# One attention and expert layer on one core: stages reordered row by row, pads zeroed up front, gate sums spread by transposes

## The chip, the cores and the metric

The kernel runs on one core of a Trainium2 chip. The core has TensorE (PE, with its weight loads PEld), VectorE (DVE), ScalarE (ACT), GpSimd (POOL) and SyncE (SP). Each of them works through a queue of its own in order, and they wait for each other on semaphores. The metric is the device time in microseconds, lower is better.

## The reference

All data is float32. `x` is 8 rows (b) of 512 tokens (t) of 128 features. Shift, scale and gain of both halves come from `silu(c) @ wmod`, and the two gains are held away from zero.

```
h   = layernorm(x) * (1 + ca) + sa                     # per row b
n   = h * rsqrt(mean(h*h) + 1e-6) * norm_w
q, k, v, o = n@Wq.T/8, n@Wk.T/8, n@Wv.T, sigmoid(n@Wo.T + bo)   # 64 wide
zi, zf = n@wi + bi, n@wf + bf                          # one number per token
scan over t:  m' = max(zf + m, zi)
              C  = exp(zf + m - m') C + exp(zi - m') v k^T ; n likewise
              out_t = o * (C q) / max(|n.q|, 1)
x   = x + ga * (h + out @ Wout.T)
h   = layernorm(x) * (1 + cb) + sb
logits = h @ Wr + br ; the two best of 8 experts, softmax of the two
x   = x + gb * sum_e gate_e * (relu(h@W1[e] + b1[e]) @ W2[e] + b2[e])
```

## The kernel before

**The attention half, row by row.** A row is 4 tiles of 128 tokens. For each row PE transposes the normalized tokens (stage `xT`, line 1213), ACT makes `hT` and its squares `sq`, PE projects (`qk` 1219, `V` 1229, `V3` 1233, the mean square `ms` 1223), DVE copies `kT` (923), POOL takes the root (`rms` 633), DVE makes `vz` (936). The scan over tokens is turned into a 512 x 512 weight matrix: PE sums the forget gates (`F` 1243, 1245), DVE forms `a_col` (943), PE spreads that column over all partitions (`abc` 1254), DVE scans for the running maximum `m_bc` (948) and adds the causal mask (`m_far` 951), ACT exponentiates (`E`), DVE multiplies with the scores (`Pw`, line 906), and PE applies the weights (`pv` 1264). Then `hh`, `hhT`, `proj` (1288), the second norm (`x1`, `ag1`, `rs1`, `xn1`), `x2T` (1294) and the router (`lg` 1301).

**The expert half, two ways.** Rows 0, 6 and 7 are dense: all 8 experts over the whole row (`du` line 1183, `dh` 697, `dd` 1192, `da` 1039; 24 pairs of a row and an expert). Rows 1 to 3 (group 0) and 4, 5 (group 1) are routed. `rank` and `pick` number the tokens of each expert, POOL scatters each token tile twice into `h_slots` in DRAM (`scat`, line 643, 8 per row), and `block_list` on DVE turns the counts into a list of 31 (23) blocks of 128 slots with one expert each. SP loads them four at a time, 14 quads in all: 4 value loads (553), 4 token blocks `xl` (555), 4 weight blocks `wl` (557). PE works through them (`T` 1146, `up` 1157, `dn` 1168), SP stores the results (563), POOL gathers them back (`gat`, line 657), DVE combines (`comb`).

**Zeros.** The last block of each expert is only partly filled. Before, `pads(g)` on SP waits for the counts, then reads 8 addresses with value loads and writes 8 zero blocks of 64 KB behind the filled slots (lines 537 to 540), twice in the program. Only the spare region behind the last expert is zeroed early (line 533).

**What sets the order.** A table `TICK` gives each step of each stage a number; each engine runs a loop over the numbers, issues what is due, and takes stages with the same number in the order of its code. The numbers set an order and nothing else. Which steps can pass each other is limited by the semaphores, and by one PSUM bank being shared by several stages (`bE` by the router, the ranks, the counts and the second norm; `bD` by `abc`, the scores, `pv` and `hhT`).

**The start.** `norm0(n)` is the first norm. It is called three times, for row 0, rows 1 to 3 and rows 4 to 7, each as one run of DVE instructions (`n0s`), followed by a power on POOL (`n0p`) and by activations on ACT for the same rows (`n0a`, line 710). `gain_diag`, `gain_rows` (PE, line 1115), `gain_out` and `gain_sum` spread the gains over partitions.

Of the kernel before, what the change touches and what calls it, by code (L numbers as in the profile page):

```python
# [5 lines left out]
def adaln_mlstm_moe_kernel(  # L6
# [67 lines left out]
    NORM0 = ((0, 1), (1, 4), (4, B))  # L74
    CAP = [len(r) * T + P for r in GROUPS]
# [10 lines left out]
    for g in range(NG):  # L86
        for p in range(0, NB[g], 2):
# [9 lines left out]
    TICK = dict(  # L97
        fill=(),
        gain_p=(47, 82),
        T=(611, 664, 703, 728, 755, 781, 831, 861, 885, 929, 978, 1012, 1038, 1071),  # L100
        up=(632, 635, 682, 685, 710, 714, 737, 740, 763, 766, 806, 820, 837, 841, 869, 873, 912, 915, 938, 941, 990, 994,
            1020, 1024, 1050, 1054, 1080, 1083),
        dn=(646, 677, 700, 705, 723, 730, 749, 757, 797, 800, 823, 833, 857, 866, 882, 889, 961, 964, 974, 987, 1005, 1008,
            1034, 1040, 1076, 1085, 1095, 1099),
        du=(267, 281, 302, 316, 328, 404, 428, 483, 875, 901, 931, 954, 967, 1013, 1027, 1057, 1088, 1113, 1127, 1141, 1155,
            1168, 1182, 1196),
        dd=(292, 309, 345, 365, 393, 416, 455, 494, 891, 922, 945, 980, 997, 1043, 1064, 1103, 1120, 1134, 1148, 1162, 1175,
            1189, 1203, 1216),
# [8 lines left out]
        F=(121, 198, 280, 402, 505, 609, 708, 809),
        S0=(138, 212, 340, 425, 526, 623, 744, 827),
        abc=(125, 202, 323, 411, 514, 613, 717, 814),
        S2=(132, 205, 338, 414, 517, 617, 721, 818),  # L120
        pv=(155, 233, 356, 444, 567, 653, 783, 848),
        hgaT=(164, 288, 372, 462, 576, 676, 791, 908),
        hhT=(175, 290, 374, 464, 587, 689, 804, 910),
        proj=(184, 299, 386, 471, 595, 696, 811, 919),
        x2T=(219, 326, 423, 503, 627, 726, 844, 952),
        lg=(241, 335, 435, 510, 639, 733, 862, 1072),
        h2=(343, 442, 519, 644, 747),
        rank=(354, 452, 533, 662, 760),
        cnt=(543, 773),
        gain_d=(42, 71, 99, 108),  # L130
        hb=(615, 668, 707, 731, 758, 801, 834, 864, 888, 933, 984, 1015, 1041, 1076),
        n0s=(53, 78),
        n0m=(52, 77, 104),
        k=(105, 176, 255, 380, 470, 588, 677, 774),
        mse=(107, 185, 263, 386, 483, 596, 680, 794),
        vz=(113, 192, 269, 393, 493, 602, 689, 803),
        a=(124, 201, 282, 406, 512, 612, 712, 812),
        scan=(133, 207, 328, 419, 521, 618, 723, 822),
# [60 lines left out]
    with ctx:  # L199
# [308 lines left out]
        def _(sp):  # L508
# [849 lines left out]
```

## Time and profile before

| what | before |
|---|---|
| time, median of 3 (lowest to highest) | 337.53 us (334.25 to 339.64) |
| profiled execution: time, span | 336.14 us, 334.3 us |
| PE busy, share of the span | 290.4 us, 87% |
| DVE, ACT, POOL busy | 193.1, 136.7, 107.9 us |
| mean granted TensorE clock | 0.904 |
| DMA traffic | 39.84 MB |

The span is the profiled execution from its first to its last instruction. Busy time of PE contains the slower stretches: a matmul at half the granted clock counts with twice its time. The row "PEclk" of the page shows that clock over 40 slices of the span, in tenths of full speed.

### The profile page before, as it was taken

The page shows a single profiled execution, that of the slowest core. Times are in us where ns is not written, and L with a number is a line of the kernel's source. Part 1 is how long each engine was busy: PE and PEld are TensorE (multiplying, and loading weights), DVE is VectorE, ACT ScalarE, POOL GpSimd, SP SyncE. Part 2 cuts the span into 40 slices and gives each one's busy share as a digit, 9 for nine tenths or more (in the row PEclk, how much of TensorE's full clock was granted, in tenths as well). Part 3 has the DMA queues.
Part 4 walks back from the last instruction along what each step waited for, and adds up shares of the span by engine and source line. Part 5 has one row for each costly group of instructions (what it writes and reads, how often), then busy time and mean ns, then how long its engine had stood idle before and what let it go on. Part 6 is the DMA issues. An engine that isn't in the chain of part 4 may idle for free.

```text
span 334.3 us, 5728 instructions
## 1 busy us (share of the span) xinstructions
PE 290.4 (87%) x1793; PEld 232.7 (70%) x1793; DVE 193.1 (58%) x769; ACT 136.7 (41%) x321; POOL 107.9 (32%) x167
## 2 busy tenths in 40 slices
PE   2662889899999999875989999999799999999992
PEld 2341568486779778645778897978688788886772
DVE  3576325542476776674576676777315565845664
ACT  1147804305462452430262675063451525443430
POOL 8024001101104704717211821730005777007730
PEclk9996557559999999965899999999999999999998
DMA  4893000000000100113246666764666487821312
GB/s 103 252 280 116 0 2 1 0 1 0 2 0 26 40 2 24 41 31 111 86 172 237 219 232 216 258 220 171 202 227 212 149 291 250 269 73 39 85 45 83
DMA packets 43315, 39.84 MB, mean 119 GB/s; under 512 B 4819, under 2 KB 34934, under 8 KB 43286
## 3 DMA queue, kind: packets, MB, share of 16 engines
q1 hardware_dynamic: 40498, 34.11, 31.2%
q0 software_dynamic: 2624, 5.31, 5.8%
q8 instruction: 14, 0.23, 0.3%
q14 instruction: 15, 0.12, 0.1%
q10 hardware_dynamic: 164, 0.07, 0.1%
HBM read 11.50 MB, written 10.22 MB: 65 GB/s over the span
## 4 chain that ended last, share of the span: by engine, by line
PE 53%; SPq 19%; DVE 11%; issue 6%; POOL 4%; DMA 4%; ACT 2%; DVEq 0%; POOLq 0%
PE bank L1192 11%; PE bank L1183 10%; PE bank L1264 6%; SPq L553 5%; SPq L557 4%; SPq L555 4%; PE bank L1123 3%; PE bank L1168 2%; PE bank L1219 2%; PE bank L1157 2%; PE bank L1254 2%; POOL yg L657 2%; SPq L522 2%; PE bank L1288 2%; POOL rstd L626 2%
## 5 line engine op out<-in xcount | busy, mean ns | idle before, releaser
L643 POOL DMA_INDIRECT h_slots<-h2k,slot x40 | 39.3, 983 | 71.7 <-DVE slot L1062 61.5
L657 POOL DMA_INDIRECT yg<-y_slots,y_slot x40 | 39.0, 975 | 57.4 <-DMA y_slots<-yb 46.0
L1192 PEld LDWEIGHTS bank<-w_all,hid_d 128*128 128x128 f32 x384 | 45.4, 192 | 8.0 <-issue 5.6
L1192 PE MATMUL bank<-w_all,hid_d 128*128 128x128 f32 x384 | 47.4, 276 | 2.1 <-DVE acc L1039 1.3
L697 ACT ACTIVATE hid_d<-bank,w_all 128x512 f32<-128x512 f32 x48 | 32.3, 691 | 33.4 <-PE bank L1183 30.5
L1183 PE MATMUL bank<-h2d,w_all 128*128 128x512 f32 x96 | 45.8, 600 | 0.0
L1039 DVE SCALAR_TENSOR_TENSOR acc<-bank,gates,acc 128x128 f32<-128x128 f32 x96 | 27.0, 344 | 26.3 <-PE bank L1192 23.3
L686 ACT ACTIVATE hid<-bank,wl 128x128 f32<-128x128 f32 x108 | 29.9, 378 | 24.4 <-PE bank L1157 23.9
L1123 PE MATMUL bank<-qT,kT 64*128 64x384 f32 (+3 forms) x64 | 28.2, 549 | 7.9 <-DVE kT L923 6.7
L1264 PE MATMUL bank<-vz,ew 128*128 128x65 f32 x160 | 25.6, 330 | 9.2 <-DVE ew L906 9.2
L1264 PEld LDWEIGHTS bank<-vz,ew 128*128 128x128 f32 x160 | 24.6, 244 | 11.7 <-DVE ew L906 11.7
L1157 PE MATMUL bank<-hb,wl 128*128 128x128 f32 x216 | 27.2, 278 | 2.2 <-issue 1.4
L1168 PE MATMUL bank<-wl,hid 128*128 128x128 f32 x216 | 28.6, 277 | 0.0
L1168 PEld LDWEIGHTS bank<-wl,hid 128*128 128x128 f32 x216 | 26.3, 192 | 3.2 <-issue 1.9
L1157 PEld LDWEIGHTS bank<-hb,wl 128*128 128x128 f32 x216 | 25.4, 192 | 4.1 <-issue 2.9
L1183 PEld LDWEIGHTS bank<-h2d,w_all 128*128 128x128 f32 x96 | 16.4, 190 | 12.7 <-issue 12.2
L1123 PEld LDWEIGHTS bank<-qT,kT 64*128 64x128 f32 x64 | 11.7, 214 | 15.2 <-issue 8.5
L633 POOL TENSOR_TENSOR rms<-ms_eps,minus_half 128x4 f32<-128x4 f32 x8 | 8.3, 1034 | 43.3 <-DVE ms_eps L928 43.2
L906 DVE SCALAR_TENSOR_TENSOR ew<-bank,rms,ew 128x512 f32<-128x512 f32 (+3 forms) x32 | 16.2, 545 | 7.4 <-PE bank L1123 3.8
L710 ACT ACTIVATE xn<-x_all,nmr,rstd 128x128 f32<-128x128 f32 x32 | 12.6, 480 | 14.9 <-DVE nmr L920 14.9
L672 ACT ACTIVATE ew<-m_far,a_col 128x128 f32<-128x128 f32 x32 | 12.5, 391 | 10.2 <-DVE m_far L951 10.2
L636 POOL TENSOR_TENSOR rstd<-ve,minus_half 128x4 f32<-128x4 f32 x8 | 8.6, 1071 | 24.0 <-DVE ve L978 23.9
(196 smaller groups left out, 454.6 us busy)
## 6 DMA issues: line engine op xcount, KB each, us to landing
wl<-w_all SPq DMA_DIRECT2D x54, 321.0 KB, 2.8
xl<-h_slots SPq DMA_DIRECT2D x54, 64.0 KB, 1.9
y_slots<-yb SPq DMA_DIRECT2D x12, 256.0 KB, 4.3
x_all<-in_L_attn_x_dram SPq DMA_DIRECT2D x8, 256.0 KB, 5.6
out_dram<-x_all SPq DMA_DIRECT2D x8, 256.0 KB, 2.6
w_all<-in_L_ffn_W_dram SPq DMA_DIRECT2D x1, 1024.0 KB, 7.5
w_all<-in_L_ffn_W_dram SPq DMA_DIRECT2D x2, 512.0 KB, 8.8
h_slots<-zeros SPq DMA_DIRECT2D x16, 64.0 KB, 1.5
```

Source lines behind the costliest of these rows:

```text
L553: words = [sp.value_load(list_w[0:1, q0 + i:q0 + i + 1]) for i in range(n)]
L643: g_.indirect_dma_start(out=h_slots[GROUP_OF[b]], out_offset=bass.IndirectOffsetOnAxis(slot[:, b, i, j:j + 1], 0), in_=h2k[m % 2][:, j, :] ...
L657: g_.indirect_dma_start(out=yg[m % 2][:, j, i, :], out_offset=None, in_=y_slots[GROUP_OF[b]], in_offset=bass.IndirectOffsetOnAxis(y_slot[: ...
L686: last = a.activation(hid[r % 2][:, m, u, :], up_at(r)[:, (m * NU + u) * P:(m * NU + u + 1) * P], ACT.Relu, bias=wl[c % RL][:, i + m, O_B1 ...
L697: a.activation(hid_d[n % 2][:, u, :], dense_banks(b)[u][:, :], ACT.Relu, bias=w_all[:, e, O_B1 + u:O_B1 + u + 1]).then_inc(s_dh, 1)
L1039: last = v.scalar_tensor_tensor(acc[:, j, :], dense_banks(b)[2][:, j * D:(j + 1) * D], gates[n // E % 2][:, j, e:e + 1], acc[:, j, :], ALU ...
L1123: t_.matmul(scores_at(j), kT[:, j * P:(j + 1) * P], qT[:, j * P:T], start=True, stop=True).then_inc(s_S, 1)
L1157: last = t_.matmul(up_at(r)[:, (m * NU + u) * P:(m * NU + u + 1) * P], wl[c % RL][:, i + m, u * P:(u + 1) * P], hb[c % 2][:, i + m, :], st ...
L1168: last = t_.matmul(y_bank[:, (i + m) * D:(i + m + 1) * D], hid[r % 2][:, m, u, :], wl[c % RL][:, i + m, at:at + D], start=u == 0, stop=u = ...
L1183: t_.matmul(dense_banks(b)[u][:, :], w_all[:, e, u * P:(u + 1) * P], h2d[:, :], start=True, stop=True).then_inc(s_du, 1)
L1192: last = t_.matmul(dense_banks(b)[2][:, j * D:(j + 1) * D], hid_d[n % 2][:, u, j * P:(j + 1) * P], w_all[:, e, at:at + D], start=u == 0, s ...
L1264: last = t_.matmul(pv_at(n), ew[:, o:o + P], vz[:, j, 0:NS], start=j == 0, stop=j == n)
```

## The change

All numbers in `TICK` are new, for every stage and engine. `norm0` and `n0a` now work one row at a time, with four semaphores for the loads of x (row 0; row 1; rows 2 and 3; rows 4 to 7) in place of three; the power on POOL stays in three groups. `pads` is gone: SP writes zeros into every slot of both groups early, 18 DMAs behind the weight loads, and the first scatter of each group waits for that group's nine. `block_list` loses the copy of the pad addresses, and its last five instructions become a stage of its own, `places`. `abc` uses transposes in place of matmuls. The rest are waits that the new order needs, and two fill stages that stay empty.

```diff
     TICK = dict(
-        gain_p=(47, 82),
-        list=(547, 777),
-        pads=(548, 798),
+        gain_p=(110, 172),
+        list=(456, 680),
+        places=(486, 952),
...
-            sp.wait_ge(s_w, 16 * (2 + NU))
-            sp.wait_ge(s_lists0, 1)
             sp.wait_ge(s_zero, 1)
             for g in range(NG):
-                sp.dma_start(h_slots[g][E * CAP[g]:SLOTS[g], :].rearrange("(n p) d -> p n d", p=P), zeros[:, :, :].to_broadcast([P, E - 1, D])).then_inc(s_spare, 16)
-
-            def pads(g):
-
-                sp.wait_ge(s_list_p, g + 1)
+
                 for e in range(E):
-                    at = sp.value_load(list_p[0:1, g, e:e + 1])
-                    sp.dma_start(h_slots[g][bass.ds(at, P), :], zeros[:, 0, :]).then_inc(s_pad, 16)
+                    sp.dma_start(h_slots[g][e * CAP[g]:(e + 1) * CAP[g], :].rearrange("(p n) d -> p n d", p=P),
+                                 zeros[:, :, :].to_broadcast([P, CAP[g] // P, D])).then_inc(s_spare[g], 16)
+                sp.dma_start(h_slots[g][E * CAP[g]:SLOTS[g], :].rearrange("(p n) d -> p n d", p=P),
+                             zeros[:, :, :].to_broadcast([P, E - 1, D])).then_inc(s_spare[g], 16)
...
+                        if b == GROUPS[GROUP_OF[b]][0]:
+                            pool.wait_ge(s_spare[GROUP_OF[b]], 16 * (E + 1))
                     g_.indirect_dma_start(out=h_slots[GROUP_OF[b]], out_offset=bass.IndirectOffsetOnAxis(slot[:, b, i, j:j + 1], 0),
...
-                for n in due("n0a", t):
-                    act.wait_ge(s_nmr, n + 1)
-                    for b in range(*NORM0[n]):
-                        for j in range(NT):
-                            last = a.activation(xn0[:, b, j, :], x_all[:, b, j, :], ACT.Identity, bias=nmr0[:, b, j:j + 1], scale=rstd0[:, b, j:j + 1])
-                        last.then_inc(s_xn0, 1)
+                for b in due("n0a", t):
+                    act.wait_ge(s_nmr, 1 + sum(1 for rows in NORM0 if rows[1] <= b))
+                    for j in range(NT):
+                        last = a.activation(xn0[:, b, j, :], x_all[:, b, j, :], ACT.Identity, bias=nmr0[:, b, j:j + 1], scale=rstd0[:, b, j:j + 1])
+                    last.then_inc(s_xn0, 1)
...
+            def norm0(b):
+                dve.wait_ge(s_x[X_SEM[b]], 16 * X_SEM.count(X_SEM[b]))
+                for j in range(NT):
+                    last = v.bn_stats(stats0[:, b, j, :], x_all[:, b, j, :])
...
                     for j in range(NT):
-                        last = t_.matmul(bD[:, j * P:(j + 1) * P], a_col[:, j:j + 1].to_broadcast([P, P]), ident[:, :], start=True, stop=True)
+                        last = t_.transpose(bD[:, j * P:(j + 1) * P], a_col[:, j:j + 1].to_broadcast([P, P]), ident[:, :])
                     last.then_inc(s_abc, 1)
```

**First place: PE in row 0.** These are PE's instructions after the setup, before the change. L1115 spreads the gains, L1123 are score products of row 0, the last row is the transposition of row 1:

```order
L1115 MATMUL bank<-diag_ga,ones 128x512 x2
L1213 MATMUL bank<-ident,xn 128x128 x4
L1219 MATMUL bank<-hT,wqk 128x512
L1229 MATMUL bank<-wvzo,hT 128x131 x3
L1115 MATMUL bank<-diag_gb,ones 128x512 x2
L1223 MATMUL bank<-mean_col,sq 128x1 x4
L1233 MATMUL bank<-wvzo,hT 128x131
L1123 MATMUL bank<-qT,kT 128x384
L1123 MATMUL bank<-qT,kT 128x128
L1213 MATMUL bank<-ident,xn 128x128 x4
```

And of the change, up to `pv` of row 0 (L1278):

```order
L1227 MATMUL bank<-ident,xn 128x128 x4
L1233 MATMUL bank<-hT,wqk 128x512
L1243 MATMUL bank<-wvzo,hT 128x131 x3
L1237 MATMUL bank<-mean_col,sq 128x1 x4
L1247 MATMUL bank<-wvzo,hT 128x131
...
L1268 MATMUL bank<-ident,a_col 128x128 x4
L1131 MATMUL bank<-qT,kT 128x256
L1227 MATMUL bank<-ident,xn 128x128 x4
L1131 MATMUL bank<-qT,kT 128x512
L1123 MATMUL bank<-diag_ga,ones 128x512 x2
L1278 MATMUL bank<-vz,ew 128x65 x10
```

Both gain products have moved behind row 0's projections: the first stands right ahead of `pv` of row 0, the second in row 1.

**Second place: DVE from the gains to row 0's `kT`.** Before:

```order
L829 TENSOR_TENSOR diag_ga<-ident,mods 128x1024
L829 TENSOR_TENSOR diag_gb<-ident,mods 128x1024
L920 SCALAR_TENSOR_TENSOR nmr<-mv,rstd 128x4
L785 BN_STATS stats<-x_all 128x6 x12
L790 BN_AGGR mv<-stats 128x2 x12
L793 TENSOR_SCALAR ve<-mv 128x12
L835 SCALAR_TENSOR_TENSOR wout_ga<-bank,woutT 64x512 x2
L920 SCALAR_TENSOR_TENSOR nmr<-mv,rstd 128x12
L785 BN_STATS stats<-x_all 128x6 x16
L790 BN_AGGR mv<-stats 128x2 x16
...
L923 COPY kT<-bank 64x512
```

Of the change (L773 and L777 are the statistics, here row 3, row 4 and row 5; those of rows 1 and 2 stand ahead of them in the same way):

```order
L913 SCALAR_TENSOR_TENSOR nmr<-mv,rstd 128x4
...
L773 BN_STATS stats<-x_all 128x6 x4
L777 BN_AGGR mv<-stats 128x2 x4
L782 TENSOR_SCALAR ve<-mv 128x12
L773 BN_STATS stats<-x_all 128x6 x4
L777 BN_AGGR mv<-stats 128x2 x4
L773 BN_STATS stats<-x_all 128x6 x4
L777 BN_AGGR mv<-stats 128x2 x4
L916 COPY kT<-bank 64x512
L921 TENSOR_SCALAR ms_eps<-bank 128x4
```

The gain diagonals have left the front, and the statistics of rows 6 and 7 and the copies of the gains stand behind `kT`.

**Third place: DVE at the first block list.** Before, the tail of the list and of `places` stands between the third and the last product of row 4's weights (L906, 128x256 and 128x128):

```order
L906 SCALAR_TENSOR_TENSOR ew<-bank,rms,ew 128x256
L858 CAST list_p<-bank 1x8
...
L884 SCALAR_TENSOR_TENSOR list_w<-blk_s,blk_m 1x31
L888 TENSOR_TENSOR blk<-end_blk,n_blk 128x8
L890 SCALAR_TENSOR_TENSOR shift_e<-blk,minus_first 128x8
L893 TENSOR_TENSOR moved<-oh,shift_e 128x192
L896 TENSOR_REDUCE move_n<-moved 128x24
L898 TENSOR_TENSOR y_slot<-slot_f,move_n 128x24
L906 SCALAR_TENSOR_TENSOR ew<-bank,rms,ew 128x128
```

Of the change:

```order
L899 SCALAR_TENSOR_TENSOR ew<-bank,rms,ew 128x256
L899 SCALAR_TENSOR_TENSOR ew<-bank,rms,ew 128x128
L850 TENSOR_TENSOR full<-bank,thr 128x96
...
L873 SCALAR_TENSOR_TENSOR list_w<-blk_s,blk_m 1x31
L1038 SCALAR_TENSOR_TENSOR acc<-bank,gates,acc 128x128 x4
L951 TENSOR_TENSOR den<-bank,rms_inv 128x4
```

The list now follows all four weight products, and `places` comes 12 rows later.

## Rows read from the trace of the kernel before

**Rows 1.** The page: the span, and PE's busy time

```profile
span 334.3 us, 5728 instructions
PE 290.4 (87%) x1793; PEld 232.7 (70%) x1793; DVE 193.1 (58%) x769; ACT 136.7 (41%) x321; POOL 107.9 (32%) x167
```

**Rows 2.** Stretches: start:end, length, busy PE, PEld, DVE, ACT, POOL, PEclk, DMA, GB/s

```profile
16.50:43.10 26.60, 15.03 (x51) 9.34 (x49) 16.57 (x79) 17.64 (x42) 6.22 (x3) 0.71 0.44 127
43.10:71.90 28.80, 26.61 (x110) 21.56 (x111) 11.40 (x39) 6.91 (x14) 2.01 (x2) 0.56 0.00 1
71.90:144.80 72.90, 70.97 (x443) 55.26 (x443) 46.64 (x212) 31.46 (x59) 21.87 (x22) 0.97 0.06 19
144.80:167.10 22.30, 15.80 (x75) 12.40 (x75) 12.48 (x50) 5.51 (x14) 8.93 (x9) 0.64 0.23 73
167.10:240.20 73.10, 68.56 (x519) 59.95 (x520) 48.06 (x192) 35.79 (x105) 21.23 (x21) 1.00 0.61 209
240.20:329.00 88.80, 86.02 (x579) 69.61 (x579) 48.01 (x157) 36.25 (x83) 40.04 (x41) 1.00 0.53 169
```

**Rows 3.** Timeline of PE: start, us, line, shapes, count, [idle before, releaser]

```profile
12.99 3.75 PE L1115 MATMUL bank<-diag_ga,ones 128*128 128x512 f32 x4 [3.01 <-DVE diag_ga L829]
31.10 2.04 PE L1123 MATMUL bank<-qT,kT 64*128 64x384 f32 x4 [6.73 <-DVE kT L923]
43.14 4.53 PE L1264 MATMUL bank<-vz,ew 128*128 128x65 f32 x20 [2.09 <-DVE ew L906]
78.06 1.88 PE L1183 MATMUL bank<-h2d,w_all 128*128 128x512 f32 x4
92.83 1.05 PE L1254 MATMUL bank<-ident,a_col 128*128 128x128 f32 x8
101.00 2.42 PE L1264 MATMUL bank<-vz,ew 128*128 128x65 f32 x20
105.10 0.60 PE L1276 MATMUL bank<-ident,h_ga 128*128 128x128 f32 x4
```

**Rows 4.** Timeline of DVE, 11 to 31 us

```profile
11.62 1.23 DVE L829 TENSOR_TENSOR diag_ga<-ident,mods 128x1024 f32<-128x1024 f32 x1
13.89 0.16 DVE L920 SCALAR_TENSOR_TENSOR nmr<-mv,rstd 128x4 f32<-128x4 f32 x1
17.18 1.65 DVE L785 BATCH_NORM_STATS2 stats<-x_all 128x6 f32<-128x128 f32 x8 [2.35 <-DMA x_all<-in_L_attn_x_dram]
25.67 1.17 DVE L790 BATCH_NORM_AGGREGATE mv<-stats 128x2 f32<-128x6 f32 x16
30.26 0.69 DVE L923 COPY kT<-bank 64x512 f32<-64x512 f32 x1
```

**Rows 5.** Timeline around the first block list, 149 to 159 us

```profile
149.91 0.14 DVE L858 CAST list_p<-bank 1x8 uint32<-1x8 f32 x1
154.47 4.53 PE L1264 MATMUL bank<-vz,ew 128*128 128x65 f32 x20 [4.97 <-DVE ew L906]
158.60 0.96 POOL L643 DMA_INDIRECT h_slots<-h2k,slot  x1 [0.30 <-issue]
```

**Rows 6.** Timeline of SP's queue: two quads' loads, the second pads

```profile
205.41 2.03 SPq L555 DMA_DIRECT2D xl<-h_slots  x4
214.45 2.00 SPq L555 DMA_DIRECT2D xl<-h_slots  x4
220.39 6.76 SPq L540 DMA_DIRECT2D h_slots<-zeros  x8
```

**Rows 7.** Zero writes: the page's list of issues, and a window over two

```profile
h_slots<-zeros SPq DMA_DIRECT2D x16, 64.0 KB, 1.5
26.90:31.00 4.10, 0.00 (x0) 0.00 (x0) 2.22 (x6) 2.22 (x6) 2.90 (x1) 0.62 0.74 224
```

**Rows 8.** Timeline of the end

```profile
320.57 0.94 POOL L657 DMA_INDIRECT yg<-y_slots,y_slot  x1 [0.30 <-issue]
326.94 2.02 PE L1192 MATMUL bank<-w_all,hid_d 128*128 128x128 f32 x16 [1.31 <-DVE acc L1039]
```

More of the change, by code:

```diff
@@ L117, in adaln_mlstm_moe_kernel @@
[L117 to L126, printed above, removed]
@@ L190, in adaln_mlstm_moe_kernel @@
+        S2=(96, 170, 256, 330, 420, 522, 632, 731),
+        pv=(124, 204, 294, 358, 456, 542, 661, 773),
+        hgaT=(136, 229, 303, 377, 465, 592, 696, 822),
+        hhT=(145, 231, 311, 379, 483, 593, 698, 832),
+        proj=(151, 237, 318, 385, 503, 602, 706, 841),
+        x2T=(179, 265, 345, 411, 559, 627, 741, 911),
+        lg=(186, 277, 354, 417, 568, 634, 748, 946),
+        h2=(284, 366, 426, 579, 641),
+        rank=(292, 372, 432, 586, 659),
+        cnt=(442, 675),
     )
@@ L348, in adaln_mlstm_moe_kernel @@
         s_w = sem("s_w")
-        s_x = [sem(f"s_xin{n}") for n in range(3)]
+        s_x = [sem(f"s_xin{n}") for n in range(4)]
         s_const = sem("s_const")
@@ L432, in adaln_mlstm_moe_kernel @@
         s_cnt = sem("s_cnt")
-        s_ls = [sem(f"s_ls{n}") for n in range(10)]
+        s_ls = sem("s_ls")
         s_list = sem("s_list")
-        s_list_p = sem("s_list_p")
         s_b0 = sem("s_b0")
@@ L441, in adaln_mlstm_moe_kernel @@
         s_zero = sem("s_zero")
-        s_spare = sem("s_spare")
-        s_pad = sem("s_pad")
+        s_spare = [sem(f"s_spare{g}") for g in range(NG)]
         s_xl = [sem(f"s_xl{n}") for n in range(RL)]
@@ L892, in block_list @@
                 each = "p r i j e -> p (r i j) e"
-                v.tensor_tensor(moved[:, 0:rows].rearrange(each), oh[:, 0:rows].rearrange(each),
+                v.tensor_tensor(moved[:, 0:rows].rearrange(each), oh[:, n0:n0 + rows].rearrange(each),
                                 shift_e[:, :].unsqueeze(1).to_broadcast([P, rows * K * NT, E]), ALU.mult).then_inc(s_moved, 1)
@@ L1069, in _ @@
                     block_list(g)
+                for g in due("places", t):
+                    block_places(g)
                 for n in due("comb", t):
@@ L1133, in _ @@
                 for n in due("fill", t):
+                    if n == 0:
+                        pe.wait_ge(s_cols, 1)
+                    keep_busy()
+                for n in due("more_fill", t):
+                    if n == 0 and EARLY:
+                        pe.wait_ge(s_dh, NU * E * EARLY)
                     keep_busy()
```

258 lines of the change are left out of this document (132 added, 126 removed).

## The prediction

> **What bounds the kernel now.** I read the page first: PE is busy for 290.4 of 334.3 us [rows 1], so PE is the engine to account for. Then I cut the span into stretches [rows 2], and the reader should take two numbers from each: how long PE idles, and at which clock it works. From 167.1 to 329.0 it idles only 4.5 + 2.8 = 7.3 us of 161.9, at full clock (2.4 GHz). From 16.5 to 167.1 it is different. 16.5 to 43.1 idles 11.6 us of 26.6; 43.1 to 71.9 is nearly full (26.61 of 28.80) but mostly at the half clock (0.56 on average); 71.9 to 144.8 is fine (1.9 us idle, clock 0.97); 144.8 to 167.1 idles 6.5 us and has 0.64. The timelines then give the reason of each hole. Up to 31.10 PE stands idle for 6.73 us waiting for `kT` [rows 3], and that copy stands on DVE behind the statistics of seven more rows [rows 4]. Ahead of 154.47 PE waits 4.97 us for the last weight product of row 4, which stands on DVE behind the block list that begins at 149.91 [rows 5]. What a half clock costs is seen from one stage at both levels: `pv` takes 4.53 us at 43.14 and 2.42 us at 101.00 [rows 3].
>
> **The sum, in four stretches.** The marks are: `pv` of row 0 starts (43.1 before), `qk` of row 2 starts (71.9), the first block transposition `T` (167.1), the last `dd` ends (329.0).
>
> *To `pv` of row 0.* The gain diagonals no longer stand ahead of `nmr`: that takes 13.89 - 11.62 = 2.3 us off the start [rows 4]. So `kT` could be copied about 2.5 us after the first projections, near 17.5, but the new order puts the statistics of rows 1 to 5 ahead of it. Rows 4 and 5 wait for the x loads, which landed at 17.18 [rows 4], and cost about 1.2 us each: 0.83 for the statistics (1.65 us for two rows), 0.3 for the aggregation (1.17 us for four), and a semaphore between them [rows 4]. I get `kT` at 19.7, against 30.26. From there the chain is the old one: from `kT` at 30.26 to `pv` at 43.14 are 12.9 us. It loses 0.9 us: `abc` falls at full clock from 1.05 us to the 0.60 of four transposes, at half clock by twice that [rows 3]. It grows by 1.6 for the first gain product, which now stands right ahead of `pv` and reaches past the 2.09 us that PE waited there (3.75 - 2.09), and by 0.5 (chosen) for the activations of rows 1 and 2, which ACT does ahead of the exponentials. 19.7 + 12.9 - 0.9 + 1.6 + 0.5 = 33.8. Gain: 9.3 us.
>
> *From `pv` of row 0 to `qk` of row 2.* Before, 26.6 us of work, mostly at half clock. The new order drops `pv` of row 1 from this stretch (4.53) and 1.0 of `abc`, and adds the second gain product and the first dense expert, some 3.75 + 3.5 us at half clock (the second an estimate, nearly twice the 1.88 us at full clock) [rows 3]. That is 28.3 us at half clock, 14 at full, plus about 3 us of waits (the root for the second norm on POOL now stands behind the power of rows 4 to 7). So 31 us if the clock stays low, 17 if it is full throughout. Two stretches of wide products (the gains) stand at the beginning, and dense work follows, but `pv` and `ms` here did not lift the clock before. I take the middle, 24. `qk` of row 2 then starts at 57.8 against 71.9. The two changes of content (one dense expert already done, one `pv` not yet) are worth 1.8 and 2.3 us and cancel. Gain so far: 14 us.
>
> *From there to the first block.* Before, 95.2 us. In them are idle time of 1.9 + 6.5 us, and the half clock, which costs half of the work done under it: a mean of 0.64 in 22.3 us and of 0.97 in 72.9 us is about 16 and 4 us at half clock, of which 11 and 4 were work, so 7 us lost [rows 2]. Now the list stands behind the weight products, and two dense `dd` and one `du` stand between rank and `pv` of row 4, so neither the 4.97 us wait nor the fall of the clock behind it should come back [rows 5]. The transposes give 4 x 0.45 = 1.8 us at full clock [rows 3]. I leave 6 us of waits in this stretch (chosen), of which over 1 us is certain: the first block waits for the last dense sum of row 0, whose `dd` now ends right ahead of it. 1.9 + 6.5 + 7.0 + 1.8 - 6.0 = 11.2. The first block starts at 167.1 - 14 - 11.2 = 142. The scatters don't hold it: after row 3's `pick` they take 8 x 1.26 us, and the first block comes 8.5 us after the last of them (158.60 to 167.1 [rows 5]), 19 us in all. Between row 3's `rank` and the first block the new order gives PE four `dd` and two `du`, `pv` of row 4 and the projections of row 5, which I count at 19 us too.
>
> *From the first block to the end of PE.* 161.9 us, less 3 x 0.45 for the transposes, less half of the 7.3 us of idle: 157.5. Before, SP spent 6.76 us on the second pads in the middle of this stretch, between two quads [rows 6]. PE was nearly full meanwhile, so only what PE idled can come back. SP still paces the blocks: a quad takes it about 9.0 us (205.41 to 214.45 [rows 6]), 13 of them 118 us, so the last quad starts at 260, and some 33 us of PE work stand behind it. That is 293, inside 142 + 157.5 = 299.5. The gathers of group 1 ended at 321.5 before, 7.5 us ahead of PE [rows 8]; they follow the last quad and move with it.
>
> Behind the last `dd` 334.3 - 329.0 = 5.3 us stay as they are [rows 8]. The span is 304.8 us. The profiled execution took 336.14 us for its span of 334.3, so 1.8 us are added: 306.6 us. The profiled execution lies 1.4 us under the median of the runs shown, and I take **306 us**, 9% less than 337.5.
>
> **The zeros.** The two groups have 14208 and 10112 slots of 512 bytes, 12.45 MB, where before 16 x 64 KB and 2 x 448 KB went out. I cost them at nothing, because before the change the DMA engines stood idle from 43 to 100 us. The bounds: the window over the two large zero writes shows 224 GB/s [rows 7], by which all takes 56 us from about 27, and group 0 is zero at 59, 20 us ahead of the first scatter at about 80. The other end is the 64 KB write, landing in 1.5 us [rows 7]: one by one that would be 44 GB/s, and group 0 zero only at 192. The new writes are large and issued back to back like those at 224 GB/s, so I take that end.
>
> **A rule against the change.** The stretch from 43.1 to 71.9 shows a low clock although PE is busy: a mean of 0.56 at 92% busy [rows 2], with many narrow products and transposes in it. The Trainium skill, "TensorE: Matmul & The Clock Gate", Part 4: PE-mode transpose, says that transposes do not count as PE work for keeping the full clock. By that rule the change takes 64 counted products out of the row chain and puts 32 uncounted ones in, and the clock would be lower for longer. Without the rule the second stretch is 24 us, with it 31 us. This is the first rival.
>
> **Rivals.**
> (a) *The clock stays low through row 1, and falls again in the row stage.* The second stretch takes 31 us, and the third loses another 5: 306 + 7 + 5 = 318 us. For it: PE at 92% busy was at 0.56 before. Against it: as soon as dense work was mixed in, the clock was 0.97 [rows 2].
> (b) *Waits of the new order.* A table made for one set of durations puts PE behind DVE or SP where it had been full. SP at 9 us a quad is nearly as long as PE's work on the first eight quads. If the whole of the old idle time comes back in the third stretch and SP's pace adds 4 us in the fourth: 306 + 3 + 4 = 313 us.
> (c) *Full clock from the first gain product on.* 17 us in the second stretch, fewer waits later: 306 - 7 - 5 = 294 us.
> (d) *No real gain.* The order brings back what it saves, in stalls of the row stage where DVE serves two rows at once: 331 to 344 us.
> (e) *The zeros come late, slower than before.* The first scatter waits for group 0, 24 scatters take 30 us, the first block comes 8.5 us behind. The kernel ends later than before once that passes about 171, so when group 0 is zero later than 132 us, which is a rate under 7.27 MB / 105 us = 69 GB/s. At the 44 GB/s of single writes the first block would come at 230, and the time would be about 395 us. Against it: 224 GB/s in the window, three times the deciding rate.
>
> **Chances.** Forecast (300 to 311) 0.38; (a) 0.20; (b) 0.17; (c) 0.17; (d) 0.05; (e) 0.03. About 2% is what a measurement of this kernel can tell from no change, that is 330.8 to 344.3 us. Faster 0.92, same 0.05, slower 0.03. The range takes (c) and (a) with the bounds of the clock: 292 to 321 us.
>
> **What the changed profile would show.** `kT` of row 0 near 20 us and `pv` near 34; no hole of 6.7 us there. If the second step is right, `qk` of row 2 starts between 51 and 65, and the clock in between says which end. The idle of PE at the first list should be under 2 us, with a clock near 1.0 from 80 to the end. The first block transposition near 142. The zero writes should fill 27 to 83 us with some 220 GB/s, with POOL's first scatter waiting for `slot` and not for them. The forecast is wrong if PE is held at half clock in the row stage, if SP's queue shows that loads start late against PE's work, or if POOL waits for the zeros.

## The result, and the profile of the changed kernel

The changed kernel takes 300.6 us (median of 4 executions, 295.86 to 306.17), the kernel before 338.58 us beside it; the ratio is 0.887, with a 95% interval of 0.854 to 0.920. Executions over 1.5% above the fastest of their kernel count as slow, and every ratio with an interval here is one of the fast ones alone, so it need not equal the ratio of the medians beside it. The profiled execution is the longest of the four (306.17 us, span 304.2). Ten more executions of it in the experiments lie between 293.88 and 312.45 us; the median of all fourteen is 301.1.

The page of the changed kernel answers to [rows 1]:

```profile
span 304.2 us, 5637 instructions
PE 282.7 (93%) x1761; PEld 225.8 (74%) x1761; DVE 194.0 (64%) x767; ACT 135.7 (45%) x321; POOL 107.1 (35%) x167
PEclk9999975957999998699799999999999999999997
PE 92%; DVE 3%; ACT 2%; DMA 1%; issue 1%; SPq 1%; DVEq 0%; ACTq 0%
```

The last row is the chain that ended last: 92% of it is PE's own work. The stretches between the prediction's marks answer to [rows 2], with the same columns: start:end, length, busy PE (count), PEld, DVE, ACT, POOL, granted clock, DMA share, GB/s.

```profile
16.50:32.91 16.41, 16.16 (x42) 9.56 (x41) 12.76 (x43) 8.39 (x20) 5.52 (x41) 1.00 0.93 251
32.91:55.68 22.77, 21.84 (x95) 14.74 (x94) 14.07 (x48) 8.22 (x18) 4.89 (x3) 0.78 1.04 284
55.68:146.06 90.38, 87.11 (x521) 68.51 (x521) 59.99 (x261) 42.31 (x88) 30.80 (x31) 0.91 0.28 84
146.06:298.86 152.80, 151.44 (x1085) 128.39 (x1085) 96.63 (x354) 72.15 (x187) 60.60 (x62) 0.99 0.56 186
```

PE idled 11.6 us in the first stretch of [rows 2]; here 0.25 us are left from 16.5 us on. From the first `pv` to the last `dd` it idles 0.93 + 3.27 + 1.36 = 5.6 us. What remains of lost time is the clock: the mean is 0.78 and 0.91 in the second and third stretch. The timelines answer to [rows 3] and [rows 4] (first DVE's `kT`, then PE):

```profile
19.63 0.69 DVE L916 COPY kT<-bank 64x512 f32<-64x512 f32 x1
```

```profile
24.10 1.11 PE L1268 MATMUL bank<-ident,a_col 128*128 128x128 f32 x4 [0.25 <-DVE a_col L936]
32.91 3.25 PE L1278 MATMUL bank<-vz,ew 128*128 128x65 f32 x20
115.60 0.60 PE L1268 MATMUL bank<-ident,a_col 128*128 128x128 f32 x4
116.87 1.06 PE L1315 MATMUL bank<-wr_sb,h2T 128*128 128x8 f32 x8 [0.66 <-ACT h2T L742]
120.78 0.36 PE L1330 MATMUL bank<-mask,tri_sr 128*128 128x32 f32 x1 [0.78 <-ACT h2k L750]
121.83 3.76 PE L1206 MATMUL bank<-w_all,hid_d 128*128 128x128 f32 x16
146.06 0.63 PE L1160 MATMUL bank<-ident,xl 128*128 128x128 f32 x4 [1.42 <-DVE acc L1038]
```

The waits of 6.73 us for `kT` and of 4.97 us at the block list are gone. `abc` takes 1.11 us at half clock and 0.60 at full. A dense `dd` that takes 2.0 us at full clock takes 3.76 at 121.83, so the clock has fallen there, behind two short waits. The zero writes (page, DMA issues: count, KB each, us to landing) answer to [rows 7]:

```profile
h_slots<-zeros SPq DMA_DIRECT2D x8, 832.0 KB, 8.7
h_slots<-zeros SPq DMA_DIRECT2D x8, 576.0 KB, 7.1
```

### The profile page after: what moved, and what is told of

The parts are those of the page before. It is cut to its first block, busy times and chain, and to the rows that moved or that the text cites. A ratio compares the mean times of both kernels' runs of the same rounds, so it can differ in the third digit from the quotient of the medians.

```text
span 304.2 us, 5637 instructions
## 1 busy us (share of the span) xinstructions
PE 282.7 (93%) x1761; PEld 225.8 (74%) x1761; DVE 194.0 (64%) x767; ACT 135.7 (45%) x321; POOL 107.1 (35%) x167
## 2 busy tenths in 40 slices
DMA packets 63794, 50.32 MB, mean 165 GB/s; under 512 B 4819, under 2 KB 55414, under 8 KB 63766
## 4 chain that ended last, share of the span: by engine, by line
PE 92%; DVE 3%; ACT 2%; DMA 1%; issue 1%; SPq 1%; DVEq 0%; ACTq 0%
PE bank L1206 15%; PE bank L1197 15%; PE bank L1131 8%; PE bank L1182 8%; PE bank L1171 8%; PE bank L1278 6%; PE bank L1302 3%; PE bank L1233 3%; PE bank L1123 2%; PE bank L1315 2%; PE bank L1237 2%; PE bank L1227 2%; PE bank L1243 2%; PE bank L1160 2%; PE bank L1268 2%; DMA wmod_sb<-in_L_wmod_dram 1%
## 5 line engine op out<-in xcount | busy, mean ns | idle before, releaser
L1206 PEld LDWEIGHTS bank<-w_all,hid_d 128*128 128x128 f32 x384 | 47.1, 197 | 7.5 <-issue 6.0
L1206 PE MATMUL bank<-w_all,hid_d 128*128 128x128 f32 x384 | 49.4, 283 | 1.3 <-DVE acc L1038 1.3
L1197 PE MATMUL bank<-h2d,w_all 128*128 128x512 f32 x96 | 47.8, 622 | 0.0
L1197 PEld LDWEIGHTS bank<-h2d,w_all 128*128 128x128 f32 x96 | 17.3, 200 | 13.4 <-issue 13.0
L1171 PEld LDWEIGHTS bank<-hb,wl 128*128 128x128 f32 x216 | 26.2, 196 | 0.7 <-issue 0.7
L1278 PEld LDWEIGHTS bank<-vz,ew 128*128 128x128 f32 x160 | 19.8, 200 | 2.0 <-issue 2.0
L1278 PE MATMUL bank<-vz,ew 128*128 128x65 f32 x160 | 19.9, 282 | 0.0
L1131 PEld LDWEIGHTS bank<-qT,kT 64*128 64x128 f32 x64 | 12.2, 219 | 6.8 <-issue 4.6
L907 DVE COPY hb<-bank 128x512 f32<-128x512 f32 (+1 forms) x14 | 9.3, 666 | 10.3 <-PE bank L1160 10.2
## 6 DMA issues: line engine op xcount, KB each, us to landing
y_slots<-yb SPq DMA_DIRECT2D x12, 256.0 KB, 3.9
x_all<-in_L_attn_x_dram SPq DMA_DIRECT2D x8, 256.0 KB, 5.8
out_dram<-x_all SPq DMA_DIRECT2D x8, 256.0 KB, 2.5
```

The lines of the kernel that those rows point to most:

```text
L1131: t_.matmul(scores_at(j), kT[:, j * P:(j + 1) * P], qT[:, j * P:T], start=True, stop=True).then_inc(s_S, 1)
L1171: last = t_.matmul(up_at(r)[:, (m * NU + u) * P:(m * NU + u + 1) * P], wl[c % RL][:, i + m, u * P:(u + 1) * P], hb[c % 2][:, i + m, :], st ...
L1197: t_.matmul(dense_banks(b)[u][:, :], w_all[:, e, u * P:(u + 1) * P], h2d[:, :], start=True, stop=True).then_inc(s_du, 1)
L1206: last = t_.matmul(dense_banks(b)[2][:, j * D:(j + 1) * D], hid_d[n % 2][:, u, j * P:(j + 1) * P], w_all[:, e, at:at + D], start=u == 0, s ...
L1278: last = t_.matmul(pv_at(n), ew[:, o:o + P], vz[:, j, 0:NS], start=j == 0, stop=j == n)
```

## What the clock costs: three executions of one program

The changed kernel was profiled three times in all. The two others have spans of 294.1 and 299.3 us. These are their last three stretches between the same marks, first of the 294.1 us execution, then of the other:

```profile
32.76:50.33 17.57, 16.31 (x95) 11.37 (x94) 13.75 (x48) 8.22 (x18) 4.89 (x3) 1.00 1.04 283
50.33:136.23 85.90, 82.62 (x522) 65.33 (x521) 60.02 (x261) 42.34 (x88) 30.76 (x31) 0.96 0.37 108
136.23:288.73 152.50, 151.19 (x1085) 128.69 (x1085) 96.59 (x354) 72.24 (x187) 60.58 (x62) 0.99 0.56 186
```

```profile
32.96:50.84 17.88, 16.62 (x95) 11.69 (x94) 13.75 (x48) 8.22 (x18) 4.89 (x3) 1.00 1.04 284
50.84:141.16 90.32, 87.17 (x521) 68.43 (x521) 60.22 (x261) 42.31 (x88) 30.45 (x31) 0.91 0.34 99
141.16:293.94 152.78, 151.46 (x1085) 128.69 (x1085) 96.73 (x354) 72.14 (x187) 60.83 (x62) 0.99 0.56 186
```

From `pv` of row 0 to the end of the last `dd` the three take 256.0, 261.0 and 266.0 us. The idle time is 5.8, 5.7 and 5.6 us. Half clock loses half of each microsecond that PE works under it, and summed over slices of 2 us that is 5.1, 10.0 and 15.1 us. What is left is 245.0, 245.3 and 245.3 us: the work at full clock. So these three executions differ by one thing, how long the clock is low: 10.2, 20.5 and 30.7 us, in two, three and four falls of 3 to 10 us each. The mean clocks of the other eleven executions agree only roughly (one at 0.961 took 295.86 us and two at the same 0.961 took 301 us), so for them this is not shown.

The same reading of the kernel before gives 285.9 us = 249.0 of work + 17.9 idle + 18.9 lost to the clock. Against the 299.3 us execution, the span of before (334.3) is 35.0 us longer: 10.2 up to `pv` of row 0, and behind it 12.2 of idle, 8.9 of clock and 3.7 of work. This split is the measure used below. The record of the granted clock leaves a part out at the start of some profiles (see the last section).

## The experiments

Every experiment ran beside the kernel before, in four groups on four chips: e1 to e4; e5b, e6b, e7b and e10b; e1c, e11 and e12; e13. Only the first and the third group had the changed kernel beside them. The others are compared with the 301.1 us of the fourteen executions, so a difference of 2 or 3 us there says nothing. Medians are over 4 executions (6 for three of them, named there).

**e1_after, e1c_after: the changed kernel again.**

> The changed kernel itself, beside the others on the same chip. Every theory expects what was measured: about 0.89 of the time before, 296 to 306 us, with qk of row 2 near 56, the first block transposition near 140 to 146, and the last dd some 153 us behind it.

> The changed kernel once more, beside the two that follow: 296 to 306 us, as its eight executions so far. All theories agree; what differs from one execution to the next is where the clock falls to half between 40 and 130 us.

Measured: 302.13 us (296.0 to 306.35), with the kernel before at 340.86; and, in the later call, 301.23 us (6 executions, 293.88 to 312.45) with before at 346.03. The medians are as expected. The marks are not all: `qk` of row 2 was expected near 56 us, as in the first profile, and came at 50.3 and 50.8, and the lowest and highest execution of the later call lie outside 296 to 306. These are the two profiles shown above.

**e2_matmul: `abc` as matmuls again.**

```diff
-                        last = t_.transpose(bD[...], a_col[:, j:j + 1].to_broadcast([P, P]), ident[:, :])
+                        last = t_.matmul(bD[...], a_col[:, j:j + 1].to_broadcast([P, P]), ident[:, :], start=True, stop=True)
```

> The new order and zeros, with abc as matmuls again. My theory: the transposes are worth what they shorten and nothing else, 8 rows by 0.45 us at full clock (1.05 against 0.60) up to 0.9 at half clock, so this kernel takes 4 to 6 us more than the changed one, about 305 us, at the same mean clock. Rival (the first rival of the prediction): transposes hold the clock down, so that with matmuls the second stretch (pv of row 0 to qk of row 2) shows a granted clock clearly above 0.78 and takes under 20 us in place of 22.8; the kernel is then as fast as the changed one or faster, 300 us or less. The Trainium skill, TensorE: Matmul & The Clock Gate, Part 4, says that transposes do not count as PE work for the full clock; by it the rival would hold.

Measured: 300.39 us, beside 302.13 for the changed kernel: no difference that the scatter lets through, and not the 4 to 6 us more of my theory. The stretches show the size:

```profile
33.26:51.33 18.07, 16.81 (x100) 11.94 (x98) 13.75 (x48) 8.22 (x18) 4.89 (x3) 1.00 1.04 283
138.21:291.95 153.74, 150.84 (x1093) 128.45 (x1093) 96.60 (x354) 72.01 (x187) 60.55 (x62) 1.00 0.56 184
```

Against the 294.1 us execution, `pv` of row 0 starts 0.5 us later (one `abc`), the second stretch is 0.5 us longer (one), the third 1.0 (four) and the last 1.2 (two): 3.2 us in sum, for eight `abc` of 0.45 us by the prediction. By the split, the work behind `pv` is 248.7 us in place of 245.0, about 0.5 us for each of seven.

The marks that the rival set for the second stretch were met: 18.07 us, at a clock of 1.00. They tell nothing, since the changed kernel, with its transposes, does the same (17.57 and 17.88 us at 1.00). The rival that transposes hold the clock down thus found no support: the clock falls in this kernel too, at 111 us behind the same work as at 110.6 in the 294.1 us execution, and its four executions have mean clocks of 0.968, 0.968, 0.930 and 0.979, where the changed kernel's fourteen have 0.924 to 0.978.

**e3_old_order: the old numbers, with the new zeros and transposes.** `TICK` is that of before, except for what the new code needs.

> The numbers of before for every stage, with the row-wise norm code, the early zeros and the transposes of the change. My theory: the order makes most of the gain. The 6.7 us wait for kT, the low clock from 43 to 72 us and most of the 5 us hole at the first list come back; what stays of the gain is 4 to 6 us for the transposes and 0 to 4 us for SP's queue without pads: 328 to 334 us, a ratio to before of 0.97 to 0.99. Rival: the zeros and the transposes make most of the gain, in that SP's queue and the clock are freed: under 318 us.

Measured: 334.8 us (332.41 to 336.77), before 340.86; the ratio is 0.994 (0.985 to 1.003). Stretches, and PE's longest waits (us in total, times, longest):

```profile
40.58:68.39 27.81, 25.66 (x106) 20.51 (x107) 11.40 (x39) 6.91 (x14) 2.01 (x2) 0.56 1.00 275
68.39:167.05 98.66, 89.47 (x506) 68.06 (x506) 58.91 (x259) 37.02 (x72) 30.70 (x31) 0.86 0.09 29
```

```profile
PE bank L1267 <- DVE ew L888: 9.1, 5, 4.8
PE bank L1120 <- DVE kT L905: 6.2, 1, 6.2
```

The three faults of [rows 2] are back: 6.2 us for `kT`, a mean clock of 0.56 behind it, 4.8 us at the list. The time lies 0.8 us above the expected 328 to 334. The order makes the gain; without it, zeros and transposes bring little.

**e4_late_pads: the new order, but pads written as before.** SP again waits for each list and writes eight blocks behind it, and the 16 early writes into the experts' slots are left out.

> The new order and the transposes, but the pads written as before: a copy of their addresses on DVE, then 8 value loads and 8 writes of 64 KB on SP behind each list (6.8 us of SP's queue each time). My theory: PE is full meanwhile and only the first one lies in the chain of the first block, so 0 to 3 us more than the changed kernel, 301 to 304 us. Rival: SP paces the blocks at 9 us a quad, and 13.5 us more in its queue come out at the end at full or half length: 307 to 314 us, with PE waiting for wl or xl in the block stage.

Measured: 314.92 us (302.9 to 319.0), with 302.13 for the changed kernel beside it: the rival held, and the median is 0.9 us above its range. One of the four executions, at 302.9, shows no loss. The rows are SP's queue, then PE (its wait in brackets), then the last stretch:

```profile
201.15 7.72 SPq L540 DMA_DIRECT2D h_slots<-zeros  x8
211.00 1.48 SPq L558 DMA_DIRECT2D xl<-h_slots  x3
```

```profile
213.97 0.87 PE L1170 MATMUL bank<-ident,xl 128*128 128x128 f32 x3 [4.59 <-DMA xl<-h_slots]
```

```profile
149.49:311.73 162.24, 154.43 (x1085) 131.21 (x1085) 96.82 (x355) 72.14 (x187) 60.58 (x62) 0.97 0.55 181
```

The first pads cost nothing, since the first block waits 1.42 us for `acc` as in the changed kernel. The second pads stand ahead of the eighth quad's loads; PE, which no longer loses time elsewhere, arrives there before them, waits 4.59 us and then works at half clock to about 219. The last stretch grows from 152.8 us (in all three profiles of the changed kernel 152.5 to 152.8) to 162.2: 6.5 us of idle and about 3 of clock. In the new order the early zeros are worth some 10 us by this profile (12.8 by the medians); with the old order they were worth little (e3).

**e5b_gains_first: the gain products at the start again.** `gain_d=(43, 68, ...)`, `gain_p=(50, 70)`.

> The changed kernel, but the two gain diagonals and their products stand at the start again, ahead of row 0's first projection, as before. My theory (first step of the prediction): DVE's two diagonals put nmr, and kT with it, 2.3 us later, near 22; the product of 3.8 us then fills PE's idle 10 to 16 us and no longer stands ahead of pv, where it reached 1.6 us past the wait. So pv of row 0 starts 0.7 us later than in the changed kernel, near 33.6, and the time is the same within 1 us. Rival: PE's idle at the start is what lets the clock fall soon after; with it filled by wide products the clock stays full from 33 us on in more executions, and the time is 3 to 6 us shorter. Other rival: the products were hidden where they stood before, and the whole 2.3 us plus a wait for kT come back, pv at 36 or later.

Measured: 311.17 us (306.43 to 314.91), before 339.32. Not the same within 1 us, and not shorter as by the first rival, but 10 us more. PE:

```profile
16.24 0.60 PE L1227 MATMUL bank<-ident,xn 128*128 128x128 f32 x4
21.34 1.96 PE L1123 MATMUL bank<-diag_gb,ones 128*128 128x512 f32 x4 [1.84 <-DVE wout_ga L824]
26.59 0.59 PE L1257 MATMUL bank<-vz,tri 128*128 128x4 f32 x2 [1.12 <-DVE vz L929]
35.26 4.53 PE L1278 MATMUL bank<-vz,ew 128*128 128x65 f32 x20 [2.09 <-DVE ew L899]
```

The wide product at 12.87 does lift the clock (four transpositions take 0.60 us at 16.24), but waits of 1.84 and 1.12 us follow, and at 26.59 PE is at half clock again. In the three profiles of the changed kernel it has left half clock by about 34 us. `pv` starts at 35.26, 2.4 us late, and 20.5 us are lost to the clock behind it, where the changed kernel loses 5 to 15.

**e12_gains_fill: the same, with seven unread matmuls in the wait ahead of `pv`.**

> The kernel with the gain products at the start, which took 311 us, with 7 unread matmuls in the wait of 2.09 us ahead of row 0's pv. The question is what the gain product was worth in its new place. My theory: it filled that wait; with the wait filled otherwise, the half clock from 35 to 62 us is gone or halved, and the time is 302 to 307 us. Rival: it is the waits between 18 and 28 us (0.87, 1.84 and 1.12 us, new with the gains at the front) that let the clock fall at 26 us, before the filled place, and it stays low till the first dense expert: 308 to 312 us.

Measured: 312.14 us (306.87 to 316.51), with 301.23 for the changed kernel beside it: the rival held. The place is filled (`pv` at 36.14, without a wait) and the clock had fallen before it. The stretch behind `pv` is shorter than in e5b (22.4 us in place of 26.1), but the time is not. So it is not the filling of that one wait that makes the gain product's new place good. That it is good because the product stands, wide, at the end of row 0, where nothing waits behind it, is a guess and not shown. It doesn't always lift the clock either: in e4 and e7b PE does the same up to `pv`, and `pv` takes the 4.37 us of half clock.

**e6b_norms_first: all first norms ahead of `kT`.** `n0s=(45, 50, 55, 62, 67, 68, 69)`, `n0m`, `n0p`, `n0a` and the first of `rms` to match.

> The changed kernel, but all first norms stand ahead of row 0's kT again, on DVE, POOL and ACT, as before. My theory: kT comes some 8 us later, near 27 to 28 (30.3 before, less the 2.3 of the diagonals), pv of row 0 near 41, and the clock falls in the idle time of 6 us, so the stretch behind takes 23 to 28 us: 8 to 13 us more than the changed kernel, 309 to 314. Rival: row 0's start is hidden behind other work of rows 1 and 2, and only 0 to 3 us of the 8 arrive at the end: 301 to 305 us.

Measured: 312.67 us (309.9 to 313.07), before 339.32: inside the 309 to 314 of my theory. PE:

```profile
27.34 2.04 PE L1131 MATMUL bank<-qT,kT 64*128 64x384 f32 x4 [6.45 <-DVE kT L916]
39.78 2.91 PE L1278 MATMUL bank<-vz,ew 128*128 128x65 f32 x20
```

`pv` comes 6.9 us later than in the changed kernel. The stretch behind it took 22.5 us, the same as in the first profile of the changed kernel, so of the two parts of my theory only the delay is shown; what else makes up the 11 us is idle (8.3 us in place of 5.7 behind `pv`, of it 2.0 us that the profile puts down to nothing and 0.8 for `xl`) and the clock (11.8 us lost, where the changed kernel loses 5 to 15).

**e7b_list_early: the first list ahead of row 4's last weight product.** `list=(454, 680)`, `places=(454, 952)`.

> The changed kernel, but the first block list with its places stands ahead of the last weight product of row 4 again. My theory: PE waits some 3 to 5 us for that product (4.97 before) in front of pv of row 4, some 2 us of it is won back where the first block no longer waits 1.42 us for acc, and the clock falls behind the wait for 1 to 4 us more: 3 to 6 us more than the changed kernel, 304 to 307 us. Rival: the two dense dd and du that now stand there cover the wait, and the list being ready earlier helps SP: 0 to 1 us, or a gain.

Measured: 310.42 us (308.04 to 315.86), before 339.32: above the 304 to 307. In the trace the cause lies as expected (PE's row, then the stretch up to the first block):

```profile
135.94 2.95 PE L1278 MATMUL bank<-vz,ew 128*128 128x65 f32 x20 [2.41 <-DVE ew L899]
```

```profile
59.35:153.99 94.64, 89.08 (x522) 69.58 (x521) 60.21 (x261) 42.31 (x88) 30.53 (x31) 0.89 0.27 84
```

`pv` of row 4 waits 2.41 us, and the stretch takes 94.6 us in place of 90.3 (the 299.3 us execution): 2.4 of idle and 2 of clock, so 4.3 us for the list. Another 8.5 us of this profile stand ahead of `qk` of row 2, where both programs have the same instructions in the same order; it is at half clock for most of the time from 22 to 56 us. Behind the first block 1.3 us come back. That the whole 9 us of the medians belong to the list isn't shown.

**e10b_holes: four pieces of PE work moved into its waits.** `dd` 435 to 413, `du` 443 to 428, `S0` and `S2` of row 5 to 515.

> The changed kernel with four places of PE moved, to fill idle time in the row stage: the fifth dense dd goes between the transposition and the router of row 3 (PE waits 0.66 us there), the seventh du between h2's transposition and the rank of row 3 (0.78 us), and the last two score products of row 5 ahead of the first block (1.42 us). My theory: the clock falls behind such idle stretches (in the changed kernel from 108 to 118 us or 120 to 127 us, at 82% busy just before), so filling them gives the 2.8 us of idle and in part of the executions the 3 to 5 us of the half clock too: 294 to 299 us, and in the profile no half clock between 100 and 130. Rival: the clock falls for another reason (narrow products and transposes), and only 1 to 3 us come: 298 to 301 us with the fall still there.

Measured: 303.67 us (302.37 to 309.24), before 339.32: no gain, and above both ranges (294 to 299, 298 to 301). PE's waits (us in total, times, longest):

```profile
PE bank L1204 <- DVE acc L1036: 2.6, 3, 1.3
PE bank L1344 <- DVE carry L1067: 1.1, 1, 1.1
PE bank L1169 <- DVE hb L905: 0.8, 1, 0.8
```

The waits of 0.66, 0.78 and 1.42 us are gone, and others of 0.46, 1.08, 0.86 and 0.76 stand in their place, for results of DVE, whose order was made for the old one. The clock falls at about 125 us all the same, behind the waits of 1.08 and 0.86 us.

**e11_fill_all: unread matmuls in all of PE's short waits.**

```diff
+        fill=(50, 50, 50, 50, 50, 50, 50, 50, 50, 50, 50, 50, 58, 58, 58, 91, 150, 150, 150, 150, 168, 168, 416, 416, 416, 416, 431, 431, 431, 431, 431, 501, 520, 520, 520, 520, 520, 520, 520, 520, 520),
...
+                    if t > TICK["du"][0]:
+                        pe.wait_ge(s_dh, NU * sum(at < t for at in TICK["du"]))
```

The two added lines make an unread matmul wait until ACT has read what the dense `du` before it wrote.

> The changed kernel, with matmuls that nobody reads (128x128, 41 in all) in the places where PE waited: 12 ahead of row 0's transposition (3.5 to 4.1 us idle), 3 ahead of its projection (0.87), then 1, 4, 2, 4, 5, 1 and 9 at the waits of 0.25 to 1.42 us of the row stage, the last ahead of the first block. They take away the idle time for the clock and nothing else, since the waits end when they did. My theory: short idle times are what lets the clock fall, and the low clock of row 0 comes from the idle time before it. Then row 0 runs at full clock from about 16 us on (abc 0.60 in place of 1.11, qk 1.1 in place of 2.07), pv of row 0 starts 4 to 7 us sooner, near 27 to 29, and no half clock stands between 30 and 150 us: 288 to 294 us. Rival: the clock falls because of what kind of work PE does (narrow products, transposes), not for lack of work: it stays as it was, and the fill costs 0 to 2 us: 300 to 304 us.

Measured: 301.71 us (6 executions, 298.77 to 307.08), beside 301.23 for the changed kernel: no gain. That is the time the rival gave, though not for its reason. Two stretches, then two waits of PE:

```profile
50.38:133.50 83.12, 82.96 (x559) 66.84 (x559) 60.45 (x261) 42.35 (x88) 30.87 (x31) 1.00 0.37 108
133.50:291.50 158.00, 153.24 (x1087) 130.68 (x1085) 96.30 (x354) 72.11 (x187) 60.64 (x62) 0.98 0.54 180
```

```profile
22.79 0.59 PE L1259 MATMUL bank<-vz,tri 128*128 128x4 f32 x2 [1.26 <-DVE vz L929]
183.54 0.63 PE L1162 MATMUL bank<-ident,xl 128*128 128x128 f32 x4 [1.24 <-DMA xl<-h_slots]
```

Half of my theory holds: from 33 to 183 us this profile shows no half clock, and the first block comes at 133.5, where the three profiles of the changed kernel have 136 to 146. Two things failed. Row 0 does run at full clock up to 22 us, but it gains nothing, because `kT` (19.59) is set by DVE; PE waits 0.84 and 1.26 us there and the clock falls at 22; `pv` starts at 32.67. And the gain ahead of the blocks is given back behind them: SP can load the first quad only once row 3's scatters have landed (its `xl` begins at 125.8, against 126.6 in the 294.1 us execution) and takes 8.6 us a quad (eight of them to 194.8), so PE waits 2.2 and 1.2 us, and the clock falls there. The last stretch grows by 5.5 us.

**e13_start: the statistics of rows 4 to 7 behind `kT`, and 27 unread matmuls.**

```diff
-        n0p=(27, 82, 151),
+        n0p=(27, 82, 254),
-        n0s=(45, 50, 55, 62, 67, 77, 129),
+        n0s=(45, 50, 55, 77, 129, 219, 234),
-        fill=(),
+        fill=(50, 50, 50, 50, 50, 50, 50, 50, 58, 58, 58, 87, 87, 87, 87, 87, 91, 150, 150, 150, 168, 416, 416, 416, 431, 431, 431),
```

The wait of e11 for `dh` is in here too.

> The changed kernel, with the statistics of rows 4 to 7 behind row 0's kT (row 4 ahead of vz, the others in rows 0 and 1), and fewer unread matmuls than in e11, in the waits of row 0, row 1 and at the router and rank of row 3, none ahead of the first block. My theory: what holds kT is DVE (two rows of statistics, 2.5 us), and with it moved kT comes near 17.5; behind it the clock is full, since PE no longer waits 0.84 and 1.26 us, so pv of row 0 starts near 30; the rest keeps its length of 245 us of work, some 5 of idle and 5 for each fall of the clock, and there are fewer falls: 293 to 298 us, a ratio to before of 0.86 to 0.875. Rival: the loads on SP's queue bound the block stage (they begin when row 3's scatters have landed and take 8.6 us a quad), and what is won ahead of them comes back as waits for xl and a fall of the clock: 298 to 302 us.

Measured: 297.85 us (6 executions, 294.82 to 300.68), before 337.7 beside it, ratio 0.886 (0.877 to 0.896): the top of my theory's range and the foot of the rival's. DVE, then PE, then the last stretch:

```profile
16.60 0.69 DVE L916 COPY kT<-bank 64x512 f32<-64x512 f32 x1
```

```profile
15.39 1.13 PE L1235 MATMUL bank<-hT,wqk 128*128 128x512 f32 x2
28.79 2.40 PE L1280 MATMUL bank<-vz,ew 128*128 128x65 f32 x20
185.13 0.63 PE L1162 MATMUL bank<-ident,xl 128*128 128x128 f32 x4 [1.74 <-DMA xl<-h_slots]
```

```profile
135.09:290.53 155.44, 150.57 (x1085) 127.67 (x1085) 96.79 (x354) 72.16 (x187) 60.66 (x62) 1.00 0.56 183
```

Both theories hold in part. The start is 4.1 us shorter (`pv` at 28.79), with row 0 at full clock up to the scores (`qk` 1.13 us, where it takes 2.07). Behind the first block PE idles 4.9 us in place of 1.3, waiting for SP. Its six executions scatter less than those of the changed kernel, and its median is 3 us under their 301.1, but it ran on another chip than they did: the ratio says no more than "at least as fast".

## Why the prediction was right, step by step

**To `pv` of row 0**: 33.8 was said, 32.9 came; `kT` 19.7 said, 19.6 came. e6b and e13 confirm that the place of the first norms sets this mark, in both directions (`kT` at 26.5 and 16.6; with unread matmuls alone, e11, it stayed at 19.6). The cost of the gain product there ("1.6 us") came out in sum, but its worth was missed: e5b puts its place at about 10 us by the medians, 2.4 of them the later `pv`, the rest mostly clock.

**`pv` of row 0 to `qk` of row 2**: 24 us said, with 17 and 31 as ends; 22.8, 17.6 and 17.9 came in the three profiles. The lower end came in two of the three. Rival (c) is thus right for this step.

**To the first block**: 84 us said, 90.4, 85.9 and 90.3 came. The 4.97 us wait is gone, and the "over 1 us" for the dense sum is the 1.42 us shown. The term that was mis-sized is the clock: 7 us were counted as recovered in full, and in every profile it falls again in this stretch (0.91 of 90.4 us is 8 us lost, 0.96 of 85.9 is 3). Idle time was overestimated: 3.3 us, where 6 were chosen.

**From the first block to the end**: 157.5 said (the terms as given make 156.9), 152.5 to 152.8 came. I let half of the idle time of [rows 2] stay; nearly all of it went (7.3 to 1.3 us). The early zeros are not enough for that: with them, but in the old order (e3), PE still idled 5.9 us from its first block on. They are needed for it: with late pads in the new order (e4) it idled 7.8.

**How near the number was.** In the profiled execution the errors nearly cancel (0.9, 1.2 and 4.7 us too much, 6.4 too little in the third stretch), and it is the longest of its four. In the two other profiles the second stretch is some 6 us shorter than said, and the median of all fourteen is 301.1. The measured 300.6 lies 0.6 us inside the 300 to 311 of the forecast, and other executions of the same kernel lie as low as 293.88, so that this narrow range held is in part luck; the wide one, 292 to 321, holds all fourteen.

**The zeros**: taken at 224 GB/s and nothing else; they ran at 284 GB/s in the second stretch, were issued between 25.4 and 66.6 us, and POOL's first scatter at 87.14 comes 0.9 us behind `slot`, as in e4, which has no such zeros to wait for. The whole traffic rose from 39.84 to 50.32 MB. But "only what PE idled can come back" was the wrong way to price the pads: it read the old order's slack. e4 shows 10 us for them once PE has caught up with SP.

**The transposes**: 0.45 us each at full clock was said, and e2 shows 0.4 to 0.5.

**The rule against the change.** The stretch behind `pv` of row 0 went from 0.56 to between 0.78 and 1.00 though 32 transposes came in. The Trainium skill, "TensorE: Matmul & The Clock Gate", Part 4: PE-mode transpose, has transposes not count as PE work. With the transposes of `abc` made matmuls again the clock fell as before (e2), so this case shows no effect of these 32 and doesn't bear the rule out; the many other transposes of the row stage were not tried.

**What stays open** is what makes the clock fall. Some falls follow short waits. The plainest case is row 3: eight profiles in the new order have the waits of 0.66 us for `h2T` and 0.78 for `h2k`, and in seven of them the clock falls right there (110.6, 115.6 and 120.8 us in the three of the changed kernel; not in e6b). In e11 and e13, where unread matmuls fill these waits, it doesn't. Other falls have no such wait ahead of them, as here in the 299.3 us execution, in row 2 and 3's narrow products, where the 294.1 us one stays at full clock:

```profile
75.73 2.47 PE L1278 MATMUL bank<-vz,ew 128*128 128x65 f32 x20
78.00 1.06 PE L1290 MATMUL bank<-ident,h_ga 128*128 128x128 f32 x4
79.43 2.07 PE L1131 MATMUL bank<-qT,kT 64*128 64x384 f32 x4
```

## What to carry to other kernels

Split PE's time into work at full clock, idle time and time lost to the clock, from two or more profiles of the same program: here the first was 245.0 to 245.3 us each time, so what was left between them was the clock, and the change itself moved mostly idle time and clock. Idle time on the path is worth more than its length, because the clock may fall behind it. And a repair can be worth little alone and much beside another: once one queue (PE) stops waiting, the next one (SP's loads) is the limit, and what was hidden in it gets its price (e3, e4).

## What the runs showed that I had not expected

One program on one chip gives 294 to 312 us (the six executions of e1c_after). In the three profiles the steps are of 5 us, by how long the clock is low.

The record of the granted clock can be wrong at the start of a program. It reads 1.00 from 16 to 33 us in the first profile while the products there take the time of half clock (`abc` 1.11 us at 24.10, 0.60 at 115.60), and in e4 up to 45 us, where `pv` takes 4.37 us. Durations of known forms tell the clock better there.

Zero writes of 576 and 832 KB from one tile ran at 284 GB/s for over 20 us without slowing PE: the second gain product takes 3.78 us at half clock with them beside it (47.24 us in the first profile) and without them (50.48 us in e4).
